# A convolution-attention and expert kernel on one core: the heads' q, k, v projections as three products of rounded and split operands

## The reference, cut to what matters

```python
# x: (4, 1024, 256) tokens after the first layer and a layer norm
h = group_norm(x) * gn_scale + gn_bias
qkv = h @ w_qkv + b_qkv                      # (4, 1024, 768), float32
qkv = qkv.reshape(B, N, H, 3, d)             # H = 8 heads, d = 32
q, k, v = (qkv[..., 0, :], qkv[..., 1, :], qkv[..., 2, :])
attn = softmax(einsum('bnhd,bmhd->bhnm', q, k) / sqrt(d))
vals = einsum('bhnm,bmhd->bnhd', attn, v)
```

## Time and profile before

| | |
|---|---|
| time, median of 3 runs | 1250.32 us (1249.89 to 1256.76) |
| profiled execution: its span | 1249.6 us; its time is recorded as this span alone, 0.7 us under the median |
| PE busy | 1141.2 us, 91% of the span |
| DVE, POOL, ACT busy | 665.9, 570.6, 424.2 us |
| convolution phase | 0 to 366 us |

### The profile page before, as it was taken

How to read it: one execution, slowest core, us unless ns; L and a number is a source line. 1 busy time by engine, 2 the same in 40 slices (tenths; PEclk the granted TensorE clock), 3 DMA queues, 4 the chain that set the end, 5 groups by cost and what they waited for, 6 DMA issues and landing times. The chain is left out here.

```text
span 1249.6 us, 23166 instructions
## 1 busy us (share of the span) xinstructions
PE 1141.2 (91%) x7476; PEld 811.9 (65%) x7477; DVE 665.9 (53%) x1481; ACT 424.2 (34%) x501; POOL 570.6 (46%) x565
## 2 busy tenths in 40 slices
PE   6899999897679999999999999998726999999995
PEld 3577677575345555555555555556615999999994
DVE  3264636444557777777777777734751333333331
ACT  1302231311115555555555555563520111111110
POOL 0003030110217888888877787860262444444443
PEclk8899999898689999999999999998957999999998
DMA  7204351304151223232232323233445556556551
GB/s 208 60 1 126 129 175 61 126 34 168 68 188 41 94 64 102 71 98 77 76 92 60 93 59 93 60 119 113 160 113 181 192 195 214 189 192 214 194 191 61
DMA packets 61607, 148.42 MB, mean 119 GB/s; under 512 B 11360, under 2 KB 31776, under 8 KB 59904
## 3 DMA queue, kind: packets, MB, share of 16 engines
q1 hardware_dynamic: 53184, 123.39, 31.0%
q0 software_dynamic: 7536, 22.96, 5.7%
q10 hardware_dynamic: 848, 1.58, 0.5%
HBM read 104.58 MB, written 39.87 MB: 116 GB/s over the span
## 5 line engine op out<-in xcount | busy, mean ns | idle before, releaser
L217 DVE TENSOR_REDUCE s_nmax<-ps_v 128x1 f32<-128x512 f32 x484 | 311.5, 685 | 114.5 <-PE ps_v L211 104.6
L923 POOL TENSOR_TENSOR h_added<-h_added,h_expd 128x1024 f32<-128x1024 f32 x124 | 295.5, 2383 | 37.5 <-ACT h_expd L946 29.6
L946 ACT ACTIVATE h_expd<-ps_v 128x1024 f32<-128x1024 f32 x128 | 131.2, 1025 | 154.9 <-PE ps_v L972 150.3
L1669 PEld LDWEIGHTS ps_h<-xs_c,lnt 128*128 128x128 f32 x1248 | 148.0, 195 | 4.8 <-issue 2.9
L1669 PE MATMUL ps_h<-xs_c,lnt 128*128 128x128 f32 x1248 | 148.4, 278 | 2.3 <-DVE xs_c L1621 2.3
L1679 PE MATMUL ps_y<-w,vals_t 128*128 x624 | 141.2, 379 | 0.6 <-DVE ys L1634 0.6
L418 POOL TENSOR_TENSOR a_res<-a_res,a_lnt 128x2048 f32<-128x2048 f32 x4 | 18.2, 4538 | 266.2 <-DVE a_lnt L123 266.2
L986 PE MATMUL h_ps_o<-h_expd,s_vh 128*32 128x256 f32 x2048 | 137.2, 385 | 0.0
L946 ACT ACTIVATE h_expd<-h_ps_e 128x1024 f32<-128x1024 f32 x128 | 130.3, 1018 | 0.0
L580 PE MATMUL a_ps_v<-a_val,a_expd 128*128 128x257 f32 x512 | 123.4, 396 | 5.1 <-ACT a_expd L458 4.5
L1710 ACT ACTIVATE vals_t<-ps_h 128x1024 f32<-128x1024 f32 x39 | 39.9, 1024 | 255.6 <-DVE ps_h L1614 255.6
(11 more groups left out here) (208 smaller groups left out, 1530.5 us busy)
## 6 DMA issues: line engine op xcount, KB each, us to landing
lnt<-in_w SPq DMA_DIRECT2D x38, 1024.0 KB, 4.9
qk_scr<-a_head_hi SPq DMA_DIRECT2D x16, 512.0 KB, 2.7
qk_scr<-a_head_lo SPq DMA_DIRECT2D x16, 512.0 KB, 3.6
w<-in_w SPq DMA_DIRECT2D x8, 1024.0 KB, 5.5
xs<-xs_scr SPq DMA_DIRECT2D x39, 128.5 KB, 2.1
a_x_t<-in_x_t POOLq DMA_DIRECT2D x4, 1024.0 KB, 9.8
r_scr<-a_res POOLq DMA_DIRECT2D x4, 1024.0 KB, 5.5
v_scr<-res SPq DMA_DIRECT2D x4, 1024.0 KB, 3.9
```

The lines of the kernel that those rows point to most:

```text
L217: self.nc.vector.tensor_reduce(self.nmax[k][:, nb, half:half + 1], ps_m[:, half, :], AX.X, ALU.max, negate=True).then_inc(self.v_max, 1)
L923: nc.gpsimd.tensor_tensor(total[:, :], (expd[:, 0, :] if m == 1 else total[:, :]), expd[:, m, :], ALU.add).then_inc(g_add, 1)
L946: nc.scalar.activation(expd[:, m, :], flat(ps_e[m % 2]), ACT.Exp, scale=SCALE).then_inc(a_exp, 1)
L1669: last = nc.tensor.matmul(ps_h[k][:, c // 4, c % 4 * P:(c % 4 + 1) * P], w1_now[k][:, t, c * P:(c + 1) * P], xs_c[:, t, :], start=(t == 0) ...
```

## The change

Each of the float32 products of `heads_qk` and `heads_v` becomes three products of float32r operands: tokens high times weights high, tokens high times weights low, tokens low times weights high (the product low times low is dropped). To that end

- ACT rounds the two weight tensors once, after the first image's values (`w_qk1s[0]`, `w_v1s[0]`), and DVE subtracts to get their low parts (`split_weights`, after `project(1)`);
- for each image ACT writes each half of `h_c` and then a rounded copy `h_hi`, and DVE writes `h_lo` (`split_h`, after the residual of `j` = 4; for the last image between two blocks of maxima);
- `h_c` gets no memory of its own: it lies on `lnt`, so ACT also waits until POOL has read `lnt` (`g_res`);
- `head_hi` and `head_lo` have two buffers instead of four. The calls `it` = 2 and 3 now wait for the spills of `it` = 0 and 1, and one semaphore `spilled` becomes two.

```diff
@@ -263,20 +263,23 @@
         ident, gmat = keep["ident"], sb("gmat", [P, P])
         w_qk0, w_v0 = sb("w_qk0", [P, CT, 2 * D]), sb("w_v0", [P, CT, C])
         w_qk1, w_v1 = sb("w_qk1", [P, CT, 4, P]), sb("w_v1", [P, CT, C])
+        w_qk1s = [sb(f"w_qk1_{x}", [P, CT, 4, P], F32R) for x in ("hi", "lo")]
+        w_v1s = [sb(f"w_v1_{x}", [P, CT, C], F32R) for x in ("hi", "lo")]
         b_qk1, gnw = sb("b_qk1", [P, 4]), sb("gnw", [P, CT, 2])
         b_v1, b_pr, gamma = sb("b_v1", [P, C]), sb("b_pr", [P, C]), sb("gamma", [P, 1])
 
         x_c, x_t = sb("x_c", [P, CT, N]), [sb(f"x_t{k}", [P, NB, C]) for k in range(2)]
         res, lnt = [sb(f"res{k}", [P, NB, C]) for k in range(2)], sb("lnt", [P, NB, C])
-        h_c = sb("h_c", [P, CT, N])
+        h_c = lnt[:, :, :].rearrange("p j c -> p (j c)").rearrange("p (t n) -> p t n", t=CT)
+        h_hi, h_lo = sb("h_hi", [P, CT, N], F32R), sb("h_lo", [P, CT, N], F32R)
 
         vhead = keep["res0"][:, :, :].rearrange("p j c -> p (j c)").rearrange("p (h j d) -> p h j d", h=NH, j=NB)
         val = [sb(f"val{k}", [P, NB, C + 1]) for k in range(2)]
         stk = [[sb(f"stk{k}{x}", [ROWS, N], F32R) for x in "nm"] for k in range(2)]
         expd = sb("expd", [P, NB, N])
         hi0, lo0 = sb("conv_hi", [2 * D, N], F32R), sb("conv_lo", [2 * D, N], F32R)
-        hi = [sb(f"head_hi{s}", [P, N], F32R) for s in range(4)]
-        lo = [sb(f"head_lo{s}", [P, N], F32R) for s in range(4)]
+        hi = [sb(f"head_hi{s}", [P, N], F32R) for s in range(2)]
+        lo = [sb(f"head_lo{s}", [P, N], F32R) for s in range(2)]
         nmax = [sb(f"nmax{k}", [P, NB, 2]) for k in range(2)]
...
@@ -362,7 +366,7 @@
                         sp.wait_ge(v_lo, 4 * b + it + 1)
                         for part, s in enumerate((hi, lo)):
                             sp.dma_start(io["qk_scr"][k, part, b * NH + g * HG:b * NH + (g + 1) * HG].rearrange("h d n -> (h d) n"),
-                                         raw(s[it][:, :])).then_inc(spilled, 16)
+                                         raw(s[it % 2][:, :])).then_inc(spilled[it % 2], 16)
                     if b + 2 < B:
                         max_rows(b + 2)
                     sp.wait_ge(v_v1, 2 * b + 2)
@@ -385,7 +389,8 @@
                 for b in range(B):
                     if b == 2:
 
-                        sp.wait_ge(spilled, 128)
+                        for s in range(2):
+                            sp.wait_ge(spilled[s], 64)
                         sp.wait_ge(v_stored, 16)
                         for j in range(EARLY):
...
@@ -462,26 +468,34 @@
                 def heads_in(b):
 
                     act.wait_ge(v_gab, b + 1)
+
+                    act.wait_ge(g_res, 2 * b + 1)
                     if b:
 
                         act.wait_ge(pe_v1, 2 * b)
                     for t in range(CT):
                         nc.scalar.activation(h_c[:, t, :], flat(ps_e[t]), ACT.Identity,
                                              scale=gab[:, 0, t:t + 1], bias=gab[:, 1, t:t + 1]).then_inc(a_h, 1)
+                        act.wait_ge(a_h, 2 * b + t + 1)
+                        nc.scalar.activation(h_hi[:, t, :], h_c[:, t, :], ACT.Copy).then_inc(a_hhi, 1)
                     for it in range(4):
                         if b == B - 1 and it == 3:
                             hd.row_hi(act, ps_v[:, 0, :], 0, 0, first=True)
                         act.wait_ge(pe_qk1, 4 * b + it + 1)
-                        if b:
-
-                            act.wait_ge(spilled, 128 * b)
-                        nc.scalar.activation(hi[it][:, :], flat(ps_e[it % 2]), ACT.Identity,
+                        if b or it >= 2:
+
+                            act.wait_ge(spilled[it % 2], 64 * b + 32 * (it // 2))
+                        nc.scalar.activation(hi[it % 2][:, :], flat(ps_e[it % 2]), ACT.Identity,
                                              bias=b_qk1[:, it:it + 1]).then_inc(a_hi, 1)
 
                 project(0)
                 for n in range(PIECES):
                     values_piece(0, n)
                 act.wait_ge(consts_in, all_consts)
+                nc.scalar.activation(w_qk1s[0][:, :, :, :].rearrange("p t g m -> p (t g m)"),
+                                     w_qk1[:, :, :, :].rearrange("p t g m -> p (t g m)"), ACT.Copy).then_inc(a_whi, 1)
+                nc.scalar.activation(w_v1s[0][:, :, :].rearrange("p t m -> p (t m)"),
+                                     w_v1[:, :, :].rearrange("p t m -> p (t m)"), ACT.Copy).then_inc(a_whi, 1)
                 for b in range(-1, B):
                     if b >= 1:
                         heads_in(b - 1)
@@ -600,20 +614,32 @@
 
                 def heads_qk(b, it):
 
-                    pe.wait_ge(a_h, 2 * b + 2)
+                    pe.wait_ge(a_hhi, 2 * b + 2)
+                    if b == 0 and it == 0:
+                        pe.wait_ge(v_wlo, 2)
                     if it >= 2:
                         pe.wait_ge(v_lo, 4 * b + it - 1)
-                    for half in range(2):
-                        for t in range(CT):
-                            last = nc.tensor.matmul(ps_e[it % 2][:, half, :], w_qk1[:, t, it, :],
-                                                    h_c[:, t, half * HALF:(half + 1) * HALF],
-                                                    start=(t == 0), stop=(t == CT - 1))
+                    products = ((0, h_hi), (1, h_hi), (0, h_lo))
+                    for i, (w, h) in enumerate(products):
+                        if i == 2 and it == 0:
+                            pe.wait_ge(v_hlo, 2 * b + 2)
+                        for half in range(2):
+                            for t in range(CT):
+                                last = nc.tensor.matmul(ps_e[it % 2][:, half, :], w_qk1s[w][:, t, it, :],
+                                                        h[:, t, half * HALF:(half + 1) * HALF],
+                                                        start=(i == 0 and t == 0), stop=(i == 2 and t == CT - 1))
                     last.then_inc(pe_qk1, 1)
 
                 def heads_v(b, q):
 
                     pe.wait_ge(v_lo, 4 * b + 3 + q)
-                    by_token(nc, ps_e[q], h_c, w_v1, q).then_inc(pe_v1, 1)
+                    for j in range(4):
+                        toks = slice((4 * q + j) * P, (4 * q + j + 1) * P)
+                        products = [(h[:, t, toks], w_v1s[w][:, t, :]) for h, w in ((h_hi, 0), (h_hi, 1), (h_lo, 0)) for t in range(CT)]
+                        for i, (h, w) in enumerate(products):
+                            last = nc.tensor.matmul(ps_e[q][:, j // 2, j % 2 * C:(j % 2 + 1) * C], h, w,
+                                                    start=(i == 0), stop=(i == len(products) - 1))
+                    last.then_inc(pe_v1, 1)
 
 
@@ -759,11 +785,26 @@
                         st.wait()
                         nc.vector.tensor_tensor(gab[:, 1, :], gnw[:, :, 1], tmp[:, 0:CT], ALU.subtract).then_inc(v_gab, 1)
 
+                def split_weights():
+                    for n, (w, s) in enumerate(((w_qk1, w_qk1s), (w_v1, w_v1s))):
+                        flat_w = lambda x: x[:, :, :, :].rearrange("p t g m -> p (t g m)") if n == 0 else x[:, :, :].rearrange("p t m -> p (t m)")
+                        dve.wait_ge(a_whi, n + 1)
+                        nc.vector.tensor_tensor(flat_w(s[1]), flat_w(w), raw(flat_w(s[0])), ALU.subtract).then_inc(v_wlo, 1)
+
+                def split_h(b):
+
+                    for t in range(CT):
+                        dve.wait_ge(a_hhi, 2 * b + t + 1)
+                        if b:
+
+                            dve.wait_ge(pe_v1, 2 * b)
+                        nc.vector.tensor_tensor(h_lo[:, t, :], h_c[:, t, :], raw(h_hi[:, t, :]), ALU.subtract).then_inc(v_hlo, 1)
+
                 def heads_qk(b, it):
 
                     dve.wait_ge(a_hi, 4 * b + it + 1)
-                    nc.vector.scalar_tensor_tensor(lo[it][:, :], flat(ps_e[it % 2]), b_qk1[:, it:it + 1],
-                                                   raw(hi[it][:, :]), ALU.add, ALU.subtract).then_inc(v_lo, 1)
+                    nc.vector.scalar_tensor_tensor(lo[it % 2][:, :], flat(ps_e[it % 2]), b_qk1[:, it:it + 1],
+                                                   raw(hi[it % 2][:, :]), ALU.add, ALU.subtract).then_inc(v_lo, 1)
 
                 def heads_v(b, q):
...
@@ -776,7 +817,7 @@
                                             ALU.add).then_inc(v_v1, 1)
 
                 precedes = {2: [(norms, 1)], 3: [(norms, 2)]}
-                follows = {0: [(norms, 0)], 5: [(heads_qk, 0), (heads_qk, 1)], 6: [(heads_qk, 2), (heads_qk, 3)],
+                follows = {0: [(norms, 0)], 4: [(lambda b, n: split_h(b), 0)], 5: [(heads_qk, 0), (heads_qk, 1)], 6: [(heads_qk, 2), (heads_qk, 3)],
                            7: [(heads_v, 0), (heads_v, 1)]}
 
                 project(0)
@@ -785,6 +826,7 @@
                 split_max(0)
                 dve.wait_ge(consts_in, all_consts)
                 project(1)
```

(4 more changed lines are left out.)

6 lines of the change are left out of this document (4 added, 2 removed).

## The result

The changed kernel takes 1239.52 us in the median of 4 runs (1237.18 to 1240.58), the one before 1250.11 (1248.88 to 1256.76), also of 4. The measured ratio is 0.9883, 95% interval 0.9857 to 0.9908; the quotient of the two medians is 0.9915, just outside it, so four runs of each do not fix the gain to better than some us. The gain is 10.6 us by the first medians, 12.6 by those of the second measurement, and the two profiled spans differ by 10.8 (1249.6 and 1238.8).

A forecast was written before the change was run, and what follows sets the result against it. PE's own work was taken to bound images 0 to 2; 13.8 us gained there plus 2.9 in the last image make 16.7, taken from the median of 1250.3 for 1233.6 us; range 1229 to 1246.

The forecast's parts named there:

- same: Whole run: the case of no change that a measurement can tell, faster meaning under 1237.8 us; chance 28%.
- The products of q and k: PE, heads_qk: 24 float32r products at 0.22 us replace eight float32 ones, gaining 1.6 us, twice per image.
- The products of v: PE, heads_v: 48 float32r products of 256 columns at 0.115 us take 5.5 us instead of 7.0, gaining 1.5.
- Costed at nothing: ACT, DVE, POOL and spills: weights' rounding, g_res wait, h_lo (0.5 us to spare) and two spill buffers cost nothing.
- The last image: Image 3, where PE, ACT and DVE hand work to each other: 2.9 us gained, bounds -1 to 5.
- the prediction's own sign: PE's brackets: prediction wrong if they name h_lo, h_hi or a DMA for more than 1 us per image.
- The four passes: ACT, last image: four passes of 1.1 us move the first q, k product from 328.70 to about 330.9.
- The second call: PE, last image, q and k: takes 2.8 us where it took 3.6, level again at 342.0.
- Third, fourth, v: Last image: third call gains 0.9 us, fourth 0.8 more; after v 1.2 remains before the phase ends.
- Loads exposed at 256 columns: PE, v: products stay at 0.215 us, 3.3 more per image than before, 1253 us in all; chance 8%.
- The reduced format not cheap: PE, heads_v: float32r runs at full four passes, 0.4375 us per product, 1296 us in all; chance 6%.
- Gain turned into waits: All images: ACT, DVE or a late spill makes PE wait 2.5 us each, 1244 us in all; chance 12%.

The follow-up runs named there:

- second measurement: The changed kernel run again unchanged, six runs, against the kernel before: ratio 0.990 (0.9881 to 0.9918).
- kernel 3: The kernel before with two spill buffers and two semaphores instead of four and one, all products float32: ratio 1.0003 to the kernel before.
- 8: The changed kernel with 26 idle float32r products put where PE waits in the last image: ratio 0.9876 to the kernel before.
- 9: The changed kernel; last image with idle products, and ACT rounding h_hi straight from PSUM while DVE makes h_c: ratio 0.9887 to the kernel before.
- 2: The changed kernel with q and k put back to float32, v keeping three products: ratio 0.9957 to the kernel before.
- 7: The changed kernel with the last image's q, k and v in float32, without its split: ratio 0.9905 to the kernel before.
- Kernel 5: The changed kernel with each v product cut into two of 128 columns, each with its own load: ratio 1.0048 to the kernel before.

## Why the prediction was right, and where it was off

**Right in mechanism.** PE bounds images 0 to 2, three float32r products cost less there than one in float32, and what is taken off PE comes off the run. The time, 1239.5, lies inside the range and 5.9 us above the forecast of 1233.6; by the profiled spans the gain is 10.8 instead of 16.7. It is above the 1237.8 under which the prediction would have called the change faster, so by its own bar the case that came is "same", to which it gave 28%, though the ratio's interval is clear of 1. Part of the agreement is luck: the low clock outside the changed places gave 2.4 us up to the last image and took 2.4 behind it, and nothing in the prediction says that these cancel.

**The products of q and k:** priced 0.22, measured 0.233 (5.60 for 24, within the 0.215 to 0.24 of the bounds). A pair gains 1.27 us, not 1.6. The choice was "nearer to the long run"; the value lies nearer to the scores' 0.24. The quarter of a float32 product, 0.215, is not what a float32r product of the same columns takes even in a long run.

**The products of v:** priced 0.115, measured 0.117 inside the run and 0.121 with the start: 5.80, not 5.5; the gain is 1.2, not 1.5. So 2 x 1.27 + 1.2 = 3.7 per image in place of 4.7. Images 0 to 2 gave 11.3 where 13.8 was forecast (bounds 9.2 to 15).

**Costed at nothing, and nothing:** the weights' rounding (ACT at 19.38, its next wait still 14.24 us long), the wait on `g_res`, `h_lo` (0.8 us to spare instead of 0.5), and the spill buffers (kernel 3). In image 2 the loss of 0.3 was put at `h_hi`; 0.2 less than in the other images was gained, and ACT ended its last pass at 265.04, with PE's first product at 265.09 and no bracket. Whether the 0.2 is that wait is not shown.

**The last image is the step that failed.** It was to gain 2.9 and loses 0.5. That lies inside the bounds of the term, -1 to 5, and their reason, ACT's passes or a colder clock, is what came; the value was wrong all the same. By the prediction's own sign, a bracket on `h_hi` of more than 1 us, this image fails too: 2.51. How late the chain is against the profile of before, at the start of each call (from the table, with the forecast's values in brackets): first call 1.9 us late (2.2), second 1.3 (0.8), third 3.2 (0), fourth 1.8 (0.9 early), heads 0.5 (2.9 early).
- *The four passes:* they took 4.48 us, as priced (4.4), and the first product is 1.9 late. Up to the second call 0.5 more was lost than forecast.
- *The second call:* forecast as level again at its end, "takes 2.8 where it took 3.6". At the full clock that is nearly right: from the second call to the third kernels 8 and 9 take 7.0 us against 7.7 before, 0.7 gained, half of a pair's 1.27. (The 3.6 is the printed length of a group and the 2.8 a pace of starts; by ACT's start it is 3.64 against 2.99.) What failed is the clock. The forecast gave the low clock to the first call and part of the third only, and it held all of the second: 5.09, so 9.6 us to the third call where 6.9 was forecast. These 2.7 us are the larger part of the 3.4 that the term is off. That the low clock is the cause is shown by the idle products (2.79 and 2.80 in kernels 8 and 9, the stage 3 us shorter in all three traces).
- *Third, fourth, v:* from the third call's start to the heads 2.7 were gained, forecast 2.9. This part was right.

The comparison itself was unlucky too. With q, k and v in float32 this stage took 56.1, 58.6 and 58.2 in three profiles, with three products 56.6 and 57.0. By their means the change gains 0.8 here, by the profile that the forecast was built on it loses 0.5. Against the other float32 profiles (2, 3 and 7: 9.4 to 9.6 us from the second call to the third) the changed kernel's 9.6 is no loss. The row from which the forecast took 3.6 was the one execution of four with that call at the full clock, and a profile cannot tell that of itself.

**The rivals.** *Loads exposed at 256 columns:* did not come; the products start 0.117 us apart and not 0.215. Kernel 5 shows that the margin is small, 0.005 us over the floor of 0.112, and what it costs to fall under it, some 20 us. The rule of the Trainium skill ("TensorE: Matmul & The Clock Gate", section "The mechanism"), that a load overlaps products in flight only when the row groups differ, would have made each product an estimated 0.21 at 256 columns; the trace does not agree. *The reduced format not cheap:* did not come, each half alone is faster. *Gain turned into waits:* no bracket of PE in images 0 to 2 names the new operands; in the last image the wait ahead of the first product grew from 0.34 (on `h_c`) to 2.51 (on `h_hi`), and the rest of the loss there is clock and no wait. The phase ended at 352.9 and not at 349, for the reasons above.

## What to carry to other kernels

Where PE is dense, three reduced products for one full one are worth 0.16 us per float32 product of 512 columns here. At 256 columns they still gain; at 128, where the load is no longer hidden, the projection of v took 10.85 us per image and so lost against the 7.00 of float32. Where PE waits for others, first ask at which clock it will run: there a shorter product may save nothing, and passes put ahead of it on ACT are paid nearly in full (1.9 us late for 2.2 more on ACT). Price a group by when its reader starts, before and after alike, and not by a printed length against a pace. Look at a stage with a wandering clock in more than one execution before building a term on it.

## What the runs showed of the hardware

- A float32r product took 0.233 us for 512 columns and 0.117 for 256, 0.456 and 0.458 ns per column, so the excess over the 0.215 of a float32 quarter goes with the columns and is no fixed cost per product. At the low clock it took 0.427 (5.12 for twelve), which is 512 columns at 1.2 GHz without any excess. What the excess is stays open.
- At 128 columns float32r products with a load of 128 columns each started 0.112 us apart, the same as the float32 records of the earlier trace rows; records with loads of 32 columns started 0.063 apart.
- The low clock of the groups of outputs behind the scores falls into different images in different executions of one kernel (3.4 to 6.6 us for the same 16 records). Two profiles differ by 1.5 to 3.2 us for each such place, and only stages free of it can be compared between them.
- In the last image 26 idle products in PE's waits brought the second call from 5.09 to 2.79 and 2.80 us in two of three traces, and to 4.25 in the third.
